# Twelve images projected by packed fp32r products, and new orders around them, in a vision block with a routed feed-forward layer

## The reference

```
q, k, v = x projected over the 64 channels by 64x64 weights and a bias, per head
ew  = exp(w_bias * mask)                        # 256 x 256
y   = sigmoid(q) * (ew @ (exp(k) * v)) / (ew @ exp(k))
h   = layernorm(y @ out_w + out_b + flatten(x)) * ln_g + ln_b
h   = concat(class token, h)                    # 257 rows per image
u   = layernorm(h);  a_t = a * sigmoid(u @ W_r + b_r)
b_t = (1 - a_t) * sigmoid(u @ W_i + b_i) * (u @ W_in + b_in)
h   = h + scan(s = a_t * s + b_t) @ W_out + b_out
v   = layernorm(h);  gates = top 2 of softmax(v @ Wr), 8 experts
out = h + ffn_shared(v) + sum of gate_e * ffn_e(v)   # ffn: 256 -> 1024 -> 256, gelu
```

## Time and profile before

| what | value |
|---|---|
| runs | 1000.52 us median of three (1000.45, 1000.52, 1001.65) |
| profiled execution | 1000.1 us, of which the span of its instructions is 998.5 |
| PE busy | 941.2 us (94%), mean granted clock 0.971 |
| DVE, ACT, POOL busy | 676.5 (68%), 458.8 (46%), 380.1 (38%) |
| first projection starts | 6.18 us, when x has arrived |
| loop of steps 4 to 15 | 106.54 to 476.90 us |
| first product of the expert phase | 553.77 us |

### The profile page before, as it was taken

One profiled execution on the slowest core, in us unless ns is written; L12 is line 12 of the kernel. 1 busy time (PEld: TensorE's weight loads), 2 busy tenths in 40 slices (PEclk: granted clock), 3 DMA queues, 4 the chain that ended last, 5 costly groups with the idle time before them and its releaser, 6 DMA issues.

```text
span 998.5 us, 21487 instructions
## 1 busy us (share of the span) xinstructions
PE 941.2 (94%) x6801; PEld 879.6 (88%) x6801; DVE 676.5 (68%) x2092; ACT 458.8 (46%) x1132; POOL 380.1 (38%) x470
## 2 busy tenths in 40 slices
PE   6879999999999999999886999999999999999996
PEld 4667898888898888988786999999999999999995
DVE  3687878877888777788887365645656456554643
ACT  2214344444444434444332455555555555555553
POOL 5272533334324243233535334342423435342322
PEclk9989999999999999999999899999999999999998
DMA  9305111011110011100025727372463826474222
GB/s 271 134 18 168 43 43 37 17 32 42 42 42 16 26 42 42 42 21 11 33 95 195 202 47 204 55 216 43 101 157 50 215 47 145 117 174 92 43 43 32
DMA packets 49187, 84.84 MB, mean 85 GB/s; under 512 B 6415, under 2 KB 30881, under 8 KB 49154
## 3 DMA queue, kind: packets, MB, share of 16 engines
q0 software_dynamic: 31056, 57.46, 23.6%
q1 hardware_dynamic: 18098, 26.96, 9.2%
HBM read 55.34 MB, written 29.09 MB: 85 GB/s over the span
## 4 chain that ended last, share of the span: by engine, by line
PE 59%; issue 21%; POOL 9%; DVE 7%; ACT 1%; POOLq 1%; DMA 0%; DVEq 0%; SPq 0%; ACTq 0%
PE ps_nd L764 17%; PE ps_proj L748 13%; PE ps_ri L748 6%; PE ps_nd L925 6%; PE ps_proj L832 5%; POOL out L709 5%; PE ps_ip L748 4%; PE ps_h L913 2%; PE ps_t L839 2%; PE ps_ip L898 2%; PE ps_t L1234 1%; POOL v_rows L524 1%; DVE E L1765 1%; POOL rstd L520 1%; DVE yb L1999 1%
## 5 line engine op out<-in xcount | busy, mean ns | idle before, releaser
L1593 DVE TENSOR_TENSOR GL<-g_act,GH 128x256 fp32r<-128x256 f32 (+1 forms) x416 | 171.3, 425 | 166.4 <-ACT GH L1293 164.9
L1288 ACT ACTIVATE g_act<-ps_proj,fcb 128x256 f32<-128x256 f32 (+1 forms) x272 | 129.5, 476 | 277.9 <-PE ps_proj L748 253.4
L764 PE MATMUL ps_nd<-w2h,GH 128*128 128x256 f32 x832 | 240.6, 289 | 2.4 <-DVE GL L1593 2.2
L764 PE MATMUL ps_nd<-w2h,GL 128*128 128x256 f32 x832 | 233.8, 281 | 0.0
L764 PE MATMUL ps_nd<-w2l,GH 128*128 128x256 f32 x832 | 232.9, 280 | 0.0
L764 PEld LDWEIGHTS ps_nd<-w2h,GH 128*128 128x128 f32 x832 | 156.3, 188 | 6.9 <-issue 1.8
L1293 ACT CAST GH<-g_act 128x256 fp32r<-128x256 f32 (+1 forms) x416 | 161.0, 401 | 1.1
L764 PEld LDWEIGHTS ps_nd<-w2l,GH 128*128 128x128 f32 x832 | 157.0, 189 | 0.0
L764 PEld LDWEIGHTS ps_nd<-w2h,GL 128*128 128x128 f32 x832 | 156.4, 188 | 0.0
L748 PE MATMUL ps_proj<-xh,w1h 128*128 128x256 f32 (+1 forms) x544 | 126.8, 315 | 10.1 <-DVE E L1765 8.7
L709 POOL DMA_INDIRECT out<-yb,rows_to x72 | 115.6, 1605 | 16.7 <-issue 14.0
(11 more groups left out here) (266 smaller groups left out, 1829.9 us busy)
## 6 DMA issues: line engine op xcount, KB each, us to landing
R<-v_rows SPq DMA_DIRECT2D x37, 260.0 KB, 2.7
w1h<-fc_w POOLq DMA_DIRECT2D x9, 1024.0 KB
w2h<-pj_w POOLq DMA_DIRECT2D x9, 1024.0 KB
stage<-fc_w POOLq DMA_DIRECT2D x9, 1024.0 KB, 11.4
stage<-pj_w POOLq DMA_DIRECT2D x9, 1024.0 KB, 13.9
v_rows<-tail_rows SPq DMA_DIRECT2D x8, 520.0 KB, 4.5
x<-x SPq DMA_DIRECT2D x16, 256.0 KB, 3.5
out<-yb SPq DMA_DIRECT2D x16, 256.0 KB, 2.1
```

The costliest lines, as they stand in the source:

```text
L764: last = pe.matmul(banks[a], g[:, j, a * P:(a + 1) * P], w[i][:, j, :], start=(j == 0 and q == 0), stop=(j == HT - 1 and q == 2))
L1288: act.activation(g_act[:, j % G_SLOTS, 0:width], banks[j % len(banks)][:, 0:width], ACT.Gelu_apprx_tanh, bias=fcb[i][:, j:j + 1]).then_inc ...
L1593: dve.tensor_tensor(GL[:, j, 0:width], g_act[:, j % G_SLOTS, 0:width], GH[:, j, 0:width].bitcast(F32), ALU.subtract).then_inc(gl_done, 1)
```

## The change

From image 4 on (PACKED = 4) a projection is made of fp32r products whose rows are packed. SP loads x twice, into partitions 0 to 63 and 64 to 127 of a buffer of 128. ACT (`x_high`) rounds both copies into XA, sorted by head. POOL (`x_low`) subtracts XA from x into XB (64 partitions, followed by rows of ones up to 97). WA holds the weights' high part over their low part, WB the high part, the bias and, in row 96, the bias's low part. Two products, XA by WA and XB by WB, replace the fp32 one. These buffers are the first expert's weight buffers, so its weights are loaded later: `next_weights` moves from step 2 to step 15 on POOL and waits for the last projection.

The class token is routed at step 2 (CLS_AFTER = 0). The lists of all engines are new; steps 14 and 15 leave the loop and are written out. PE gets eight `spare` pieces in the opening, each two fp32 products into `ps_ri` whose result nobody reads. The limits are read in two parts on PE, the transposes of the first block between them, and the WARM products go.

```diff
+    KB = 97
+    PACKED = 4
-        X = [sb(f"x{i}", [KA, LH]) for i in range(2)]
+        X = [sb(f"x{i}", [P, LH]) for i in range(2)]
+        XA = [W1L[1][:].rearrange("p k n -> p (k n)")[:, i * LH:(i + 1) * LH] for i in range(2)]
+        XB = [W2L[1][:].rearrange("p j m -> p (j m)")[0:KB, i * LH:(i + 1) * LH] for i in range(2)]
+        WA = W1H[1][:, 0, :]
+        WB = W1H[1][0:KB, 1, :]
-        CLS_AFTER = NIMG - 2
+        CLS_AFTER = 0
                 sp.dma_start(X[par][0:C, :], x[n]).then_inc(x_loaded[par], 16)
+                if packed:
+                    sp.dma_start(X[par][C:2 * C, :], x[n]).then_inc(x_loaded[par], 16)
+            def x_low(t, par):
+                n = t + 1
+                if live(n):
+                    p = 1 - par
+                    pool_wait(pool, xq_done, n - (PACKED - 1), "xq")
+                    pool.tensor_tensor(XB[p][0:C, :].rearrange("c (h l) -> c h l", h=H),
+                                       X[p][0:C, :].rearrange("c (l h) -> c h l", h=H),
+                                       XA[p][0:C, :].rearrange("c (h l) -> c h l", h=H).bitcast(F32),
+                                       ALU.subtract).then_inc(xs_done, 1)
             def next_weights(t, par):
+                pool.wait_ge(proj_ready, LT * NIMG)
...
             def project(n, par, lt):
+                    if packed:
+                        cols = slice(h * 4 * D, (h + 1) * 4 * D)
+                        pe.matmul(ps_proj[:, h, :], packed_view(XA[par], lt, h), WA[:, cols],
+                                  start=True, stop=False)
+                        last = pe.matmul(ps_proj[:, h, :], packed_view(XB[par], lt, h),
+                                         WB[:, cols], start=False, stop=True)
...
+            def spare(t, par, k):
+                pe.wait_ge(consts, CONSTS)
+                for _ in range(2):
+                    pe.matmul(ps_ri[:, 1, :], ones_pp[:], zeros[:, 0, :], start=True, stop=True)
...
-            limits = block_limits(pe)
-            for _ in range(WARM):
-                pe.matmul(ps_t[:, 0, :], ones_r[:], W2H[0][:, 0, :], start=True, stop=True)
+            limits = [0] + block_limits(pe, 1, AHEAD)
             transpose_rows(0)
+            limits += block_limits(pe, AHEAD, NE + 1)
...
+            def x_high(t, par):
+                    act.copy(XA[p].rearrange("c (h l) -> c h l", h=H),
+                             X[p][:].rearrange("c (l h) -> c h l", h=H)).then_inc(xq_done, 1)
...
+            def pack_split(t, par):
+                dve.tensor_tensor(wproj_h, wproj[:].rearrange("c h d -> c (h d)"),
+                                  wproj_h.bitcast(F32), ALU.subtract).then_inc(pack_low, 1)
...
             with pe.Fori(PEEL // 2, NIMG // 2 - 1) as pair:
```

More of the change, by code:

```diff
@@ new lines, in mixer_tensor @@
+            hidden(14, 0, 2)
+            hidden(14, 0, 3)
+            hidden(14, 0, 4)
+            rank(14, 0)
+            turn_u(14, 0)
+            sums0(14, 0)
+            sums1(14, 0)
+            hidden(14, 0, 5)
+            gates0(14, 0)
+            turn_v(14, 0)
+            hidden(14, 0, 6)
+            gates1(14, 0)
+            ffn_out(14, 0, 0)
+            input0(14, 0)
+            turn_y(15, 1)
+            hidden(14, 0, 7)
+            input1(14, 0)
+            h_out(15, 1)
@@ L2091, in mixer_vector @@
             u_norm(3, 1)
-            gate_b(2, 0)
-            u_low(3, 1)
-            low(3, 1, 1)
-            bias_wait(2, 0)
-            ratio0(3, 1)
-            ratio1(3, 1)
             low(3, 1, 2)
@@ new lines, in mixer_vector @@
+            u_norm(14, 0)
+            v_norm(14, 0)
+            low(14, 0, 0)
+            low(14, 0, 1)
+            u_low(14, 0)
+            low(14, 0, 2)
+            places(14, 0)
+            ratio0(14, 0)
+            ratio1(14, 0)
+            y_last(14, 0)
+            low(14, 0, 3)
+            low(14, 0, 4)
+            slots_out(14, 0)
+            v_low(14, 0)
+            low(14, 0, 5)
+            gate_a(14, 0)
+            h_sum(15, 1)
+            low(14, 0, 6)
+            h_norm(15, 1)
@@ L2117, in mixer_vector @@
+            gate_b(14, 0)
+            ekv0(15, 1)
+            best(15, 1)
+            u_stats(15, 1)
+            low(14, 0, 7)
+            ekv1(15, 1)
+            u_norm(15, 1)
+            base_sum(14, 0)
+            second(15, 1)
+            v_sum(15, 1)
+            u_low(15, 1)
+            low(15, 1, 0)
+            ratio0(15, 1)
+            low(15, 1, 1)
+            v_norm(15, 1)
+            ratio1(15, 1)
+            v_low(15, 1)
             ekv0(16, 0)
+            y_last(15, 1)
@@ L2118, in mixer_vector @@
             ratio0(16, 0)
-            h_sum(16, 0)
+            low(15, 1, 2)
+            low(15, 1, 3)
+            ratio1(16, 0)
+            places(15, 1)
+            low(15, 1, 4)
+            slots_out(15, 1)
+            low(15, 1, 5)
+            y_last(16, 0)
+            low(15, 1, 6)
+            h_sum(16, 0)
+            ekv1(16, 0)
+            low(15, 1, 7)
+            best(16, 0)
+            h_norm(16, 0)
+            gate_a(15, 1)
+            u_stats(16, 0)
+            second(16, 0)
```

768 lines of the change are left out of this document (481 added, 287 removed).

## The result

The changed kernel takes 988.83 us (median of four runs, 987.18 to 992.9) beside 1001.09 for the kernel before in the same session (four runs, 1000.45 to 1002.37): a ratio of 0.988, 95% interval 0.985 to 0.991. It is faster, by 12 us and not by 32; 969 was forecast, and the range ended at 982. The profiled run took 988.81, of which the span is 987.2.

What follows compares the result with a forecast made beforehand. PE (TensorE) was taken to set the loop. Projection -17.8, opening -4, drain -6 and between the phases -3 summed to -30.8, a span of 967.7; the forecast time was 969 us, range 954 to 982.

Steps and rivals of the forecast that it cites:

- The opening: Images 0 to 3 entering: net -4 us from moved splits, class token's routing and spare products; ends -15 and +6.
- the prediction's own sign: Stated in advance for the opening: the prediction is wrong if the opening takes longer than 106.5 us.
- The projection: Loop: packed fp32r products take 1.88 us per image in place of 3.36, -1.48 each, -17.8 us over 12 images.
- The added work: Loop: ACT's rounding (about 1.2 us), POOL's subtraction (about 2.5) and SyncE's second copy cost 0; other end 1.6 per image.
- DVE's new order: Loop: h's norm now stands behind E; DVE has 0.9 us to spare, so the order costs 0.
- The clock: Loop: short products and the wait remain, so seven falls of twelve stay; ends -11.5 us (none) or +8 (all).
- the first rival: More is gained: denser projection keeps the clock up, or the opening closes its waits; likeliest 957 us; chance 0.14.
- The drain: After the loop: -6 us from the class token's wait and records going and half the split's cost; ends -11 and 0.
- the start: Between the phases: limits read in two parts, no warming, 6.35 us in place of 10.4; -3, ends -4 and +1.
- GpSimd holds DVE: Rival, loop: 0.8 to 1.6 us per image over 12 images, 979 to 988 us; chance 0.15.
- Slower than before: Rival, loop: the four-element-step subtraction takes 5 us, falls on the GL differences and holds DVE; 1018 us; chance 0.03.

Runs made afterwards that it cites:

- the first experiment: Changed kernel with the kernel before's lists for steps 0 to 3 and 16 to 18, packing's pieces put in; 980.27 us, 0.976 to 0.982 of the kernel before.

## Why the prediction failed, step by step

- **The opening, -4 forecast, +12.0 found.** This is the step that failed; the prediction's own sign, an opening longer than 106.5, came true. "The eight pairs of spare products meet 21 us in which PE is idle: 0": five of them do, the three behind the first `turn_y` cost 4.5. "Both splits now stand earlier, I count the 2.9 us of the hold and 2.5 of the clock": w2l's split now stood beside the scan. The hold grew, and a stretch at the lower clock followed it; both splits together cost 5.9 there, and with w2l's beside the reciprocals 3.5 of it come back. Nor was the old place worth 5.4: placing the splits well in the old opening gives 3.1. I had asked whether the old place was left, not which instruction of DVE lies at the new one. Of the 12.0, the spare products are 4.5, w2l's place 3.5, the packing's own pieces 1.2 to 1.8; the other 2.2 to 2.8 lie in the rest of the new order and stay open. The class token's routing, which I charged 2.2, cost nothing beside the held scan; whether it is in those 2.2 to 2.8, no run shows.
- **The projection, -1.48 per image.** Right in its mechanism and somewhat larger. The two groups of eight packed products take 1.05 and 1.07 to the next instruction's start. The fp32 ones took 1.97 behind the transposes and 1.68 behind `attention`; I had used the 1.68 of the earlier trace rows for both. That makes 1.53. Between the new step with fp32 and with packed products but no subtraction it is 29.83 for 27.96, 1.9; the 0.3 beyond the products I did not trace.
- **The added work at 0 with the other end 1.6.** Found 0.5. The place beside the reciprocals was as forecast and the hold is short there; ACT and POOL were underestimated (2.08 and 2.91), as a read with a step of four elements was in no row of before.
- **DVE's new order at 0.** With fp32 products it is 0, as I said (29.8 and 29.9 an image without a fall). With packed ones the order decides: with the same ends the packed kernel takes 1023.6 in the old step and 980.3 in the new. The old step was tried with one place of the subtraction alone.
- **The clock, seven falls kept.** Wrong, in the kernel's favour: one of ten images in the profiled run, none to three in the other kernels with this packed step. This gain is luck as far as the forecast goes; only the first rival named one, by the denser projection, and that is not the cause by itself. Neither the packing alone (in the old step six of twelve images fall with the subtraction, nine without it) nor the order alone (six of twelve) does it; both together do. Which property of the pair keeps the level, I can't say: PE's wait is 0.68 in both new steps. That stays open.
- **The loop's sum.** Steps 4 to 13 fell by 22.5: ten times 1.9, five falls of 1.65 less, ten times 0.5 more make 22.2. The last two steps, written out, are 61.5 for 61.1, so the packing gained nothing there; with the step of the loop in their place, as in the first experiment, they take 57.9.
- **The drain, -6, and the start, -3.** Found -0.8 together (drain 67.1 for 66.5, start 8.9 for 10.4). The splits cost 4.0 of it. The gain that I counted for the class token's move, 4.7, is not shown: moving it back into these lists made them 12.7 longer, but the old lists, with the routing late, take 76.9 with the limits in two parts, and 74.1 with the splits placed. The new lists I did not take apart further. The limits in two parts gave 3.8 with the old ends.
- **The rivals.** "GpSimd holds DVE" was right as a mechanism and wrong in place: it is the opening's loss and the drain's, and 0.5 per image in the loop. That its 979 to 988 lies near the result is a coincidence, since it put the whole loss into the loop. "Slower than before" came true in the packed kernel with the old step, by that very hold: its images are 1.6 to 1.7 longer than before's at either clock.
- **The whole.** The opening is 16.0 worse than forecast and drain and start 8.2 worse; the loop is 4.3 better, mostly by the clock. Either of the first two alone would have left the time inside the range; together they put it outside, and the clock's luck made the miss smaller.

The Trainium skill, "SBUF — State Buffer", section "SBUF: two separate sides", gives the lock of the shared port pair to DVE operations in a 2-port perf mode too, not only to those with two SBUF inputs. The prediction used the second half alone. The rows agree with both: a tensor_scalar of two columns held for 2.80 beside a subtraction of 2.89, a cast of eight for 5.32, a reciprocal from PSUM not at all. In which mode an instruction ran, no row tells.

## What to carry to other kernels

When elementwise work moves on GpSimd, list the instructions that VectorE will have beside it at the new place, small ones included: one that takes 0.17 us alone can be held until GpSimd's ends (2.80 here), and a chain stands behind it. Reciprocals from PSUM are a good cover, reached by a wait on the right semaphore. A shorter product can lengthen the wait behind it (1.13 for 0.68 in the old step), and the clock can then fall in more images; so test a packing and its order together. Filler products are free only where PE would have waited as long anyway: test them by taking them out, piece by piece. And when a change brings new lists for the ends as well as for the loop, try the loop's part with the old ends: here that alone gave 980.3, with the limits in two parts 974.4, and with the splits placed 968.7, where the whole change gave 988.8.

## What the runs showed that I had not expected

- A COPY of 128x2 took 1.19 us and a TENSOR_SCALAR of 128x2 2.80 beside GpSimd's subtractions; alone they take 0.17. Neither has two tensors from SBUF.
- ScalarE's copy of 128x1024 with a step of four elements took 2.08 us; 128x512 without one 0.64. GpSimd's subtraction of 64x1024 with that step took 2.91; 128x1024 without one 2.35.
- Two changes, each worth nothing or less alone (1023.6 and 1001.6), were worth 20 us together (980.3).
- Beside two subtractions of GpSimd in a row, the first scan in the drain was held through both (4.42 us), while in the opening each scan was held by one (2.47 and 2.76).
